# The last layer's stack loads in another order on the sync queue of a recurrent and attention kernel

## The reference

```
# attention: 16 heads of 8 features, a bias that falls with distance
qkv = x @ qkv_w.T + qkv_b                     # split into q, k, v
scores = einsum('bhid,bhjd->bhij', q, k) / sqrt(8) - abs(i - j) * 0.5**h
attn = softmax(scores, axis=-1)
s = einsum('bhij,bhjd->bhid', attn, v) @ out_w.T + out_b

# mixture: each of 16 experts takes the 160 tokens with the highest top-1 gate
top1_val, top1_idx = softmax(x @ Wg).max, .argmax
vals, idx = top_k(where(top1_idx == n, top1_val, -inf), 160)
y[idx] = gelu(x[idx] @ W1[n] + b1[n]) @ W2[n] + b2[n]   # other tokens keep x
x = x + s * silu(y)
```

## Time and profile before

| | us |
|---|---|
| median of 3 runs | 1933.77 |
| lowest and highest | 1930.42, 1935.26 |
| profiled execution, its own time | 1933.77 |
| its span in the profile | 1931.3 |
| PE busy | 1562.3 (81%) |
| DVE busy | 1178.2 (61%) |
| ACT busy | 1016.9 (53%) |
| POOL busy | 208.8 (11%) |

### The profile page before, as it was taken

How to read it: one execution, slowest core, us unless ns; L and a number is a source line. 1 busy time by engine, 2 the same in 40 slices (tenths; PEclk the granted TensorE clock), 3 DMA queues, 4 the chain that set the end, 5 groups by cost and what they waited for, 6 DMA issues and landing times. The chain is left out here.

```text
span 1931.3 us, 23980 instructions
## 1 busy us (share of the span) xinstructions
PE 1562.3 (81%) x8656; PEld 782.9 (41%) x8656; DVE 1178.2 (61%) x2370; ACT 1016.9 (53%) x1658; POOL 208.8 (11%) x152
## 2 busy tenths in 40 slices
PE   5999999987798688977888778984785677877886
PEld 2556555554454344433444334432222322322442
DVE  4789999899846733367434665236216777675522
ACT  4787787774042167532675336662772123334675
POOL 1343342432000000000000000000000000001003
PEclk9999999999899799868899799886566567889988
DMA  4433232353110300203002020006012212022002
GB/s 163 119 78 76 78 80 74 83 182 77 60 51 17 99 18 1 82 1 99 19 1 82 17 82 19 17 1 203 25 33 77 71 35 76 14 65 58 1 2 71
DMA packets 91621, 116.30 MB, mean 60 GB/s; under 512 B 10096, under 2 KB 71536, under 8 KB 91120
## 3 DMA queue, kind: packets, MB, share of 16 engines
q1 hardware_dynamic: 89808, 110.05, 20.0%
q0 software_dynamic: 1696, 4.72, 0.8%
HBM read 83.27 MB, written 31.46 MB: 59 GB/s over the span
## 5 line engine op out<-in xcount | busy, mean ns | idle before, releaser
L1665 ACT ACTIVATE scratch<-ps 128x1024 f32<-128x1024 f32 x272 | 270.8, 1022 | 212.7 <-PE ps L1267 68.4
L2079 DVE TENSOR_REDUCE neg_max<-ps 128x2 f32<-128x1024 f32 (+2 forms) x224 | 234.4, 1068 | 106.5 <-PE ps L1211 105.5
L1648 ACT ACTIVATE ps<-ps 128x512 f32<-128x512 f32 x256 | 150.1, 586 | 84.4 <-PE ps L1257 84.0
L1936 DVE TENSOR_TENSOR_SCAN scratch<-scratch 128x512 f32<-128x512 f32 x128 | 159.5, 1286 | 2.7 <-ACT scratch L1619 2.4
L1844 DVE SCALAR_TENSOR_TENSOR gated<-tanh,ps 128x512 f32<-128x512 f32 x88 | 60.4, 687 | 144.0 <-ACT tanh L1547 143.9
L1547 ACT ACTIVATE tanh<-ps 128x512 f32<-128x512 f32 x88 | 52.3, 595 | 160.8 <-PE ps L992 160.5
L1311 PE MATMUL ps<-scratch,values 128*32 128x512 f32 (+3 forms) x1024 | 130.1, 600 | 3.0 <-ACT scratch L1665 1.5
L1027 PE MATMUL ps<-xnt,weights_even 128*128 128x512 f32 x256 | 125.8, 613 | 7.4 <-ACT gated L1530 6.6
L2259 POOL TENSOR_SCALAR variance_eps<-mean_var 128x4 f32<-128x4 f32 x20 | 5.3, 264 | 1006.8 <-DVE mean_var L1764 1006.8
L992 PE MATMUL ps<-xnt,weights_odd 128*128 128x512 f32 x176 | 111.8, 721 | 0.0
L1665 ACT ACTIVATE weights_even<-ps 128x1024 f32<-128x1024 f32 x64 | 65.1, 1023 | 81.0 <-PE ps L1274 77.2
(11 more groups left out here) (323 smaller groups left out, 2955.9 us busy)
## 6 DMA issues: line engine op xcount, KB each, us to landing
scratch<-state_rows SPq DMA_DIRECT2D x64, 512.0 KB, 4.8
scratch<-parts_scratch SPq DMA_DIRECT2D x288, 96.0 KB, 2.4
parts_scratch<-weights_even SPq DMA_DIRECT2D x168, 128.0 KB, 2.4
weights_odd<-in_l SPq DMA_DIRECT2D x8, 519.5 KB, 6.5
weights_even<-in_l SPq DMA_DIRECT2D x1, 4096.0 KB, 16.2
weights_odd<-in_l SPq DMA_DIRECT2D x1, 4096.0 KB, 13.9
parts_scratch<-gated SPq DMA_DIRECT2D x15, 128.0 KB, 2.4
slots_scratch<-head_out SPq DMA_DIRECT2D x5, 256.0 KB, 5.0
```

The source lines that it names most:

```text
L1648: ins = act.activation(bank, bank, ACT.Exp, accum_out=dens[:, j, h:h + 1])
L1665: act.activation(dst, src, ACT.Exp).then_inc(q[l, "exp_done"], 1)
L1936: dve.tensor_tensor_scan(hs[:, g, :], da[n % RING][:, g, :], ub[:, g, :], 0.0, ALU.mult, ALU.add)\
L2079: ins = dve.tensor_reduce(dst, ps[:, base:base + 2, col:col + n], AX.X, ALU.max, negate=True)
```

## The change

Two edits, both in the code of SP for layer 3.

First, inside `last_stacks` the loops are exchanged. Before: quad by quad, and for each the three stacks. Now: stack by stack, and for each the four quads. The wait for `b_ready` goes with the quad into the inner loop, and the one wait of batch 0 for layer 2 stands before the third stack.

Second, `last_stacks(b)` for b = 2 and 3 is issued whole. Before, quads 0 to 2 came first, then the maxima of batch b - 1, then quad 3. Now all four quads come first, and then the maxima of batch b - 1.

```diff
-            def last_stacks(b, quads=range(QUADS)):
+            def last_stacks(b):
                 l = 3
-                for g in quads:
-                    if b > 1:
-                        sp.wait_ge(q[l, "b_ready"], start[l, "b_ready"] + NUB[l] * (b - 2) + quad_end(l, g))
-                    for s in range(3):
-                        if b == 0 and s == 2 and g == 0:
-                            sp.wait_ge(q[2, "b_ready"], NUB[2] * NB - 8)
+                for s in range(3):
+                    if b == 0 and s == 2:
+                        sp.wait_ge(q[2, "b_ready"], NUB[2] * NB - 8)
+                    for g in range(QUADS):
+                        if b > 1:
+                            sp.wait_ge(q[l, "b_ready"], start[l, "b_ready"] + NUB[l] * (b - 2) + quad_end(l, g))
                         k = min(s, 1)
...
             last_stacks(1)
-            maxima(3, 0)
-            for b in range(2, NB):
-                for n in range(2):
-                    part_out(3, b, n)
-                last_stacks(b, range(QUADS - 1))
-                maxima(3, b - 1)
-                last_stacks(b, range(QUADS - 1, QUADS))
-            maxima(3, NB - 1)
+            for b in range(NB):
+                maxima(3, b)
+                if b + 2 < NB:
+                    for n in range(2):
+                        part_out(3, b + 2, n)
+                    last_stacks(b + 2)
```

## The result

The changed kernel takes 1965.51 us (median of 4 runs, 1960.14 to 1971.06), against 1934.51 us before in the same comparison: a ratio of 1.0166, with an interval of 1.0136 to 1.0197. In a later comparison, with 6 more runs, it took 1971.04 us against 1932.65, a ratio of 1.0197 (1.0166 to 1.0228). It is slower, by 31 to 38 us. The forecast was 1966 us in a range of 1955 to 1974.

The account below looks back on a forecast made before the run. PE together with DVE and ACT was taken to bound layer 3's sections, with loads hidden. Added to 1933.77 us, 0.5 + 12.7 + 1.0 + (12.7 + 4.2) + 1.0 = 32.1 gave 1966 us, range 1955 to 1974.

Parts of the forecast that it names:

- That the maxima fall behind the burst, and that PE stops at B(1, 0) and B(2, 0) for them: At both seams of layer 3, SP issues 18 transfers before the maxima; PE's queue stands still until the maxima land.
- The first pause, 12.7 us late: Seam at 1655.88: 9.4 us of issues plus 4.5 to PE's start, making B(1, 0) 12.7 us late (10.8 to 13.0).
- The second pause, 12.7 + 4.2 = 16.9: Seam at 1754.30: the same 12.7 us, plus 4.2 (0 to 5.2) because POOL's read of all slots delays the maxima.
- The exchange of the loops, 0.5 us for A(0, 0): Batch 0: quad 0 of all three stacks is complete at the 18th transfer, not the 6th; 0.5 us late (0 to 1).
- The clock after a pause, 1.0 us each: Behind each seam PE restarts about 5 us at the lower clock, costing 1.0 us a seam (0 to 2.5).
- my clock rival: Clock stays down, both later sections at section 1's pace: 3 + 5 = 8 us instead of 2, total 1972; chance 0.10.
- the sign that I had named: What would show it: the sections themselves, without the pauses, keep their length within a few microseconds.
- The sum, 32.1 us: Loop exchange, two pauses, slots' delay and two clock restarts together add 32.1 us to the profiled 1933.77.
- The other side: Rival at the seams: burst is early enough and maxima land under cover, nothing lost, 1934 us; chance 0.03.

Follow-up runs that it names:

- quad 3 first: From the kernel before, only quad 3's loads put ahead of the maxima, loops as they were: 1957.75 us, ratio 1.0127.
- Loops only: From the changed kernel, quad 3 put back behind the maxima, so only the loops are exchanged: 1938.21 us against 1933.91, ratio 1.0014.

## Why the prediction was right, step by step

*That the maxima fall behind the burst, and that PE stops at B(1, 0) and B(2, 0) for them:* right, and shown by PE's waits. SP starts the 18 transfers when B(0, 31) ends (1652.69 and 1652.72), six having gone ahead.

*The first pause, 12.7 us late:* 11.5 measured, within its ends of 10.8 and 13.0. The round trip from the issue of the maxima to PE was taken at 4.5 us and is 4.3. The issues were taken at 9.4 and are 8.4: 0.47 us each, between the low row of 0.447 and my 0.52.

*The second pause, 12.7 + 4.2 = 16.9:* 15.2 measured. Its contention, taken at 4.2, is 3.4 to 4.0 by the kernel with the slots moved. The maxima's way out took 2.0 us at the first seam and 4.9 at the second, where I had expected about 6. But I had the wrong thing in front of them. The issue of the slots by POOL, and from issue to landing the slots, the last transfer of SP's burst (issued at 1778.72) and the maxima:

```profile
1768.50 1.36 POOL L2273 DMA_DIRECT2D weights_even<-slots_scratch  x1 [1.57 <-DMA slots_scratch<-xn,logits]
...
weights_even<-slots_scratch POOLq DMA_DIRECT2D x1, 1280.0 KB, 9.2
...
scratch<-parts_scratch SPq DMA_DIRECT2D x1, 96.0 KB, 5.2
max_scratch<-xnt_sequence SPq DMA_DIRECT2D x1, 32.0 KB, 4.9
```

The slots, issued 0.6 us behind SP's start in the kernel before, now went out 1.4 us ahead of it. They had landed at 1768.50 + 9.2 = 1777.7, and the maxima were issued at 1779.19, 1.5 us later. What was still under way was SP's own burst: its last transfer landed at 1783.9, and the maxima 0.2 us behind it. So the slots work through the burst. They share the DMA engines with it, its 18 transfers take 6.1 us to land (median) in place of 2.4 at the first seam, and the maxima come behind these. With the slots moved away the maxima again land 0.2 us behind the last of the burst, after 2.1 us.

The rule cited from the Trainium skill ("DMA: Bandwidth & Descriptors", "Queues, rings and completion order") agrees with that: no trace has the maxima landing ahead of the burst, or of slots whose read was issued before them. It bears on the slots themselves in *quad 3 first*, where the maxima were issued at 1769.43, 5.0 us ahead of the landing of the slots, and landed at 1775.65, 1.2 us behind it. The runs don't tell the order of the semaphore's write from plain sharing of the DMA engines.

*The exchange of the loops, 0.5 us for A(0, 0):* nothing. A(0, 0) starts at 1466.08, and the transpose ahead of it on PE, which needs no stack, is later by the same 0.24 us. The low end was right; the burst was issued a little faster than I had counted (24 in 11.49 us). *Loops only* has nothing against it in the total.

*The clock after a pause, 1.0 us each:* this is the term that was mis-sized. The direction was right. The stretches behind the first pause, columns as in the earlier trace rows:

```profile
1655.00:1660.00 5.00, 0.00 (x0) 0.00 (x0) 0.00 (x0) 0.00 (x0) 0.00 (x0) 0.74 0.70 207
1660.00:1665.00 5.00, 0.00 (x0) 0.00 (x0) 0.00 (x0) 0.00 (x0) 0.00 (x0) 0.50 0.35 107
1665.00:1670.00 5.00, 4.58 (x23) 1.04 (x23) 0.87 (x1) 1.03 (x2) 0.00 (x0) 0.50 0.00 0
1670.00:1675.00 5.00, 5.00 (x29) 1.13 (x28) 4.02 (x11) 1.47 (x2) 0.00 (x0) 0.56 0.00 0
1675.00:1680.00 5.00, 3.34 (x32) 1.83 (x30) 4.16 (x7) 1.60 (x2) 0.00 (x0) 1.00 0.02 3
```

The clock fell to its lower level of 1.2 GHz in the pause and stayed there for nearly 10 us of work, not 5. The price of the restart is 2.9 us at the first seam: B(1, 3) comes after 11.50 us where it came after 8.62, and filling the pause takes exactly that back up to this unit. Over the whole of section 2 the stretch was 7.4 us, with the mean clock at 0.74 (105 us) where it was 0.84 (97 us) in the earlier trace rows. So my clock rival, with 3 us for this section, was nearer in kind and too small in size, and the sign that I had named, sections that keep their length within a few microseconds, failed for section 2. I had judged the cost of a section at a lower clock by section 1, which does other work and varies by 4 us in itself (97.0 to 101.3). The Trainium skill, "TensorE: Matmul & The Clock Gate", "HAM oscillation — how this bites in real kernels", had the mechanism (half rate after a wait for a transfer, paid at each such wait), and the trace agrees for the restart. The 4.6 us of the last six units are not the restart.

*The sum, 32.1 us:* 31.4 in the profiled span. That it is so near is partly luck. My pauses were 2.9 us too long together and the exchange 0.5. Section 2 was 7.4 us longer and section 3 by 3.5, where I had put 1.0 each. The 6 us that section 1 and the rest were shorter, lengths that vary by as much between traces of one kernel (section 1 98.1 and 100.9, the rest 71.5 and 79.7 in the changed one), took most of that back. The second traces of both kernels differ by 44.4 us, and in other parts: 11.7 and 15.8 us of pauses, 4.8 in section 2, 9.3 in section 3. What the runs show as made by the change, the pauses and section 2, is 32 to 34 us in both pairs. How much of section 3 is made by it stays open, and so does what made the second comparison 38 us.

*The other side* is excluded: SP's burst starts at the unit's end in every trace with one.

What stays open: why the clock is at its lower level for most of the last six units of section 2 behind a pause, filled or not, more than 80 us after it, and in none of the four traces without one. That the clock's changes are set off by how the work happens to lie is a guess, and wasn't isolated. None of the kernels is faster than the kernel before.

## What to carry to other kernels

In a queue that is issued in order, ask of each transfer that waits what stands behind it, and who needs that. Here a load without hurry waited for the last unit of a batch, and the first unit of the next needed the small transfer behind it, so all of the load's issue time became idle time of TensorE. Count such a pause as issues times issue time plus the round trips, and add what the first units behind it lose at the lower clock. Another queue's large read beside the burst delays what stands at the burst's end, even when that read has landed before. Here the section behind the first pause lost 2.6 to 4.7 us more in its last units, which no row of the kernel before would have told. And look at a second trace before giving a few microseconds of a section to a change: here sections that the change can't reach varied by 3 to 4 us.

## What the runs showed of the hardware

- Behind an idle time of TensorE of 7.1 to 12.9 us at the first seam the next three units took 2.8 to 2.9 us longer (five traces), and behind 11.9 to 17.8 us at the second seam 1.5 to 3.2 us (five traces). The granted clock there was 0.50.
- The section of 97 us behind the first seam took 4.9 to 7.4 us longer in all, for a pause of 7.1 us (104.3) as much as for one of 12.7 (104.5).
- 42 matmuls in a wait kept the clock at 1.00 while they ran. After the 3.78 us of idle time behind them it was at 0.50 at the restart and for the next 5 us and more, as after 12.7 us of idle time.
- Issuing one of these 96 KB transfers from SP took 0.47 us in a burst of 18 after a wait, and 0.51 us beside the read of 1280 KB.
- A transfer of 32 KB to DRAM took 1.9 to 2.3 us right behind a burst of 6 or 18 of its own queue, and 4.9 to 6.2 us behind such a burst that ran beside another queue's read of 1280 KB, also where that read had landed before the 32 KB were issued. With nothing ahead it was 1.5 to 1.7 us, but 3.2 and 3.4 in two traces at the first seam.
